# Soft mixture layer: logits computed once with slots on partitions, token maxima from transposed raw tiles, combine weights exponentiated in place later, dispatch turned tile by tile

## What is computed

```python
def _L1_ffn_ref(x, phi, w1, b1, w2, b2):       # x (4, 512, 192), phi (4, 256, 192)
    logits = jnp.einsum('bnd,esd->bnes', x, phi)
    B, N, E, S = logits.shape
    dispatch = jax.nn.softmax(logits, axis=1)
    combine = jax.nn.softmax(logits.reshape(B, N, E * S), axis=-1).reshape(B, N, E, S)
    slots = jnp.einsum('bnd,bnes->besd', x, dispatch)
    h = jax.nn.gelu(jnp.einsum('besd,edh->besh', slots, w1) + b1[None, :, None, :])
    y = jnp.einsum('besh,ehd->besd', h, w2) + b2[None, :, None, :]
    out = jnp.einsum('besd,bnes->bnd', y, combine)
    return out
...
t = t + _L1_ffn_ref(_ln_t(t), phi, w1, b1, w2, b2)
```

## Time and profile before

| | us |
|---|---|
| median of three runs | 1077.12 |
| the three runs | 1083.49, 1074.96, 1077.12 |
| the profiled execution | 1087.93 |
| its span on the core | 1086.2 |

### The profile page before, as it was taken

One profiled execution on the slowest core, in us unless ns is written; L12 is line 12 of the kernel. 1 busy time (PEld: TensorE's weight loads), 2 busy tenths in 40 slices (PEclk: granted clock), 3 DMA queues, 4 the chain that ended last, 5 costly groups with the idle time before them and its releaser, 6 DMA issues.

```text
span 1086.2 us, 15072 instructions
## 1 busy us (share of the span) xinstructions
PE 974.2 (90%) x5552; PEld 772.5 (71%) x5552; DVE 530.0 (49%) x1021; ACT 470.3 (43%) x919; POOL 107.7 (10%) x193
## 2 busy tenths in 40 slices
PE   3788878888888887999989889999999999999998
PEld 2655665576557555887767676899689967997798
DVE  5767668865877676343354455203520353026200
ACT  6655355563545554332244345332542164216321
POOL 3012002100400001123142000000000000000000
PEclk9889979996899999998599999999999999999999
DMA  6001000000000001000000020000000000000000
GB/s 170 1 1 34 2 0 10 23 0 0 29 0 1 1 1 33 10 10 20 19 26 13 1 103 1 1 1 14 0 0 0 14 0 0 0 15 1 0 1 15
DMA packets 12709, 15.45 MB, mean 14 GB/s; under 512 B 5313, under 2 KB 10561, under 8 KB 12545
## 3 DMA queue, kind: packets, MB, share of 16 engines
q1 hardware_dynamic: 10656, 9.46, 2.9%
q0 software_dynamic: 2016, 5.51, 1.8%
HBM read 13.39 MB, written 1.57 MB: 14 GB/s over the span
## 4 chain that ended last, share of the span: by engine, by line
PE 70%; DVE 19%; issue 5%; ACT 4%; DMA 1%; SPq 0%; DVEq 0%; POOL 0%; ACTq 0%; POOLq 0%
PE ps L210 22%; PE ps L1299 11%; PE ps L1054 7%; DVE room L564 6%; PE ps L1275 5%; PE ps L1311 4%; DVE area L262 3%; PE ps L1119 3%; PE ps L1035 3%; ACT area L801 2%; DVE nm L553 2%; PE ps L1168 2%; PE ps L933 2%; PE ps L1253 1%; PE ps L953 1%
## 5 line engine op out<-in xcount | busy, mean ns | idle before, releaser
L210 PE MATMUL ps<-xs,ws 128*128 128x512 f32 x460 | 122.9, 419 | 12.2 <-DVE xs L473 8.1
L564 DVE RECIPROCAL room<-ps 32x224 f32<-32x224 f32 (+1 forms) x72 | 97.1, 1348 | 70.5 <-PE ps L1054 55.1
L1299 PE MATMUL ps<-area 128*128 128x192 f32 x768 | 127.4, 326 | 0.0
L1299 PEld LDWEIGHTS ps<-area 128*128 128x128 f32 x768 | 124.9, 190 | 2.0
L210 PE MATMUL ps<-ws,wx 128*128 128x512 f32 x480 | 116.0, 397 | 1.2 <-DVE ws L689 1.2
L699 DVE TENSOR_TENSOR area<-ps,area 128x384 f32<-128x384 f32 x32 | 17.8, 558 | 196.4 <-PE ps L1299 196.4
L210 PEld LDWEIGHTS ps<-xs,ws 128*128 128x128 f32 x460 | 89.3, 200 | 33.9 <-issue 9.3
L801 ACT ACTIVATE area<-ps,nm 112x196 f32<-112x196 f32 (+1 forms) x240 | 85.6, 435 | 60.7 <-DVE nm L553 60.7
L210 PEld LDWEIGHTS ps<-ws,wx 128*128 128x128 f32 x480 | 89.2, 188 | 22.6 <-DVE ws L689 2.9
L905 ACT ACTIVATE area<-ps,bcol 128x512 f32<-128x512 f32 x96 | 65.6, 688 | 86.6 <-PE ps L210 86.5
L1054 PE MATMUL ps<-area,room 98*64 98x224 f32 x384 | 88.9, 378 | 12.0 <-DVE area L569 12.0
(11 more groups left out here) (148 smaller groups left out, 1407.4 us busy)
## 6 DMA issues: line engine op xcount, KB each, us to landing
stage<-in_wall POOLq DMA_DIRECT2D x42, 128.0 KB, 2.4
area<-in_w2e SPq DMA_DIRECT2D x1, 2304.0 KB, 8.4
out<-xres SPq DMA_DIRECT2D x4, 384.0 KB, 2.6
xres<-in_x SPq DMA_DIRECT2D x1, 1152.0 KB, 7.1
area<-in_wall SPq DMA_DIRECT2D x2, 512.0 KB, 6.1
area<-in_w2a SPq DMA_DIRECT2D x1, 576.0 KB, 4.0
room<-in_rel SPq DMA_DIRECT2D x4, 128.0 KB, 5.5
xres<-in_x SPq DMA_DIRECT2D x1, 384.0 KB, 3.1
```

Of the source, the lines that this page charges most:

```text
L210: last = mm(out_, l, r, start=n == 0, stop=n == len(pairs) - 1)
L564: V.reciprocal(dn, ps[32:64, 6, 0:n]).then_inc(a_own, 1)
L1299: last = mm(ps[:, 4 + b, s * D:s * D + D], hTd[:, m, b * T + s * P:b * T + s * P + P], w2x[:, e * MC + m, :], start=m == 0, stop=m == MC - 1)
```

## The change

The token logits are gone. Each slot tile s is computed once, slots on partitions, into banks 0 to 3 in turn, and copied raw to `ct` (ScalarE for even s, VectorE for odd). From there three things go on.

- VectorE takes its two maxima out of SBUF, ScalarE its exponentials into a ring of four `dt_` tiles, VectorE the reciprocals, and GpSimd multiplies. TensorE transposes each tile as it comes, three steps behind its product, into banks 6 and 7, from where VectorE (even) and ScalarE (odd) copy it to `dd`.
- TensorE transposes the raw tile too (banks 4 and 5), and VectorE takes the maxima over its slots (`pm`), then over the tiles (`nrm`, negated). Four more transposes of a broadcast operand spread these maxima over the partitions, and VectorE copies them to `bc`.
- GpSimd adds `bc` to the eight raw tiles, and ScalarE takes their exponentials in place after the last gelu. The row sum comes from a column of ones in `yy`: the last product is 193 columns wide, and VectorE takes the reciprocal of that column ahead of the residuals.

The groups of tokens to slots are ordered by slot half; the first one is issued ahead of the last tile's transposes. The removed lines of the `body_d` functions are left out here, since they stand in the functions above.

```diff
-        (cc, _, ct, dt_, w2x, b2row) = views([(2, NE * NS), (1024,), (ST, N), (2, ST, T), (NE * MC, D), (NE, D)])
-        dd = cc, dt_[:, 0].rearrange("p s t -> p (s t)").rearrange("p (j c) -> p j c", j=2)
-        yy = area[:, 0:2 * ST * D].rearrange("p (b s d) -> p b s d", b=2, d=D)
-        dstart = 2 * NE * NS + 1024 + ST * N
-        hTd = area[:, dstart:dstart + MC * N].rearrange("p (a b) -> p a b", b=N)
+        (dd, dt_, _, ct, bc, w2x, b2row) = views([
+            (2, 2, NE * NS), (4, 2, T), (ST * 2,), (ST, N), (N,), (NE * MC, D), (NE, D)])
+        yy = area[:, 0:2 * ST * (D + 1)].rearrange("p (b s d) -> p b s d", b=2, d=D + 1)
+        hTd = area[:, 2 * ST * (D + 1):2 * ST * (D + 1) + MC * N].rearrange("p (a b) -> p a b", b=N)
...
+            def dispatch_combine(n):
+                for s in range(ST):
+                    pool.wait_ge(d_rc, n * ST + s + 1)
+                    nc.gpsimd.tensor_tensor(dt_[:, s % 4], dt_[:, s % 4],
+                                            rcs[:, 2 * s:2 * s + 2].unsqueeze(2).broadcast_to([P, 2, T]), ALU.mult)\
+                        .then_inc(d_dn, 1)
+                pool.wait_ge(d_bc, n + 1)
+                for s in range(ST):
+                    nc.gpsimd.tensor_tensor(ct[:, s, :], ct[:, s, :], bc, ALU.add).then_inc(d_cs, 1)
...
                 for n in range(PAIRS):
+                    if ph == 3 and n:
+                        dispatch_combine(n - 1)
...
+            dispatch_combine(PAIRS - 1)
...
+                for s in range(ST + 3):
+                    if s < ST:
+                        if s % 2:
+                            dve.wait_ge(d_l, it * ST + s + 1)
+                            V.tensor_copy(ct[:, s, :], ps[:, s % 4, :]).then_inc(d_rv, 1)
+                        dve.wait_ge(d_rv if s % 2 else d_ra, it * 4 + s // 2 + 1)
+                        V.tensor_reduce(ncm[:, 2 * s:2 * s + 2], ct[:, s, :].rearrange("p (b t) -> p b t", b=2),
+                                        AX.X, ALU.max, negate=True).then_inc(d_ncm, 1)
+                    if 1 <= s <= ST:
+                        v = s - 1
+                        dve.wait_ge(d_dt, it * ST + v + 1)
+                        V.reciprocal(rcs[:, 2 * v:2 * v + 2], csum[:, 2 * v:2 * v + 2]).then_inc(d_rc, 1)
+                        dve.wait_ge(d_rt, it * ST + v + 1)
+                        V.tensor_reduce(pm[:, :, v], ps[:, 4 + v % 2, :].rearrange("p (n c) -> p n c", c=P),
+                                        AX.X, ALU.max).then_inc(d_pm, 1)
+                    if s == ST:
+                        dve.wait_ge(d_pm, it * ST + ST)
+                        V.tensor_reduce(nrm[:], pm, AX.X, ALU.max, negate=True).then_inc(d_nm, 1)
+                    if s >= 4 and s % 2 == 0:
+                        dve.wait_ge(d_dtr, it * ST + s - 3)
+                        V.tensor_copy(dd[:, :, :, (s - 4) * P:(s - 3) * P],
+                                      ps[:, 6 + s % 2, :].rearrange("p (b j c) -> p b j c", b=2, c=P)).then_inc(d_de, 1)
+                dve.wait_ge(d_bt, it + 1)
+                V.tensor_copy(bc, ps[:, 4, :]).then_inc(d_bc, 1)
+                for h in range(2):
+                    for b in range(2):
+                        dve.wait_ge(d_sh, it * 4 + 2 * h + b + 1)
+                        bank = 4 * h + 2 * b
...
-                        V.tensor_tensor(yy[:, b, 2 * e:2 * e + 2, :],
+                        if e + b == 0:
+                            V.memset(yy[:, :, :, D:D + 1], 1.0)
+                        V.tensor_tensor(yy[:, b, 2 * e:2 * e + 2, 0:D],
                                         ps[:, 4 + b, 0:2 * D].rearrange("p (s d) -> p s d", d=D),
...
+                        front_split(it + (3 * PAIRS + 1), NT, (d_l, ST * it + ST))
+                for k in range(2):
+                    dve.wait_ge(d_o, 1 + it * 2 + k + 1)
+                    po = ps[:, 6 + k, 0:2 * (D + 1)].rearrange("p (t c) -> p t c", c=D + 1)
+                    V.reciprocal(rrs[:, 2 * k:2 * k + 2], po[:, :, D]).then_inc(d_own, 1)
+                    dve.wait_ge(d_own, it * 2 + k + 1)
+                    for t in range(2):
+                        xt_ = xres[:, it * NT + 2 * k + t, :]
+                        V.scalar_tensor_tensor(xt_, po[:, t, 0:D], rrs[:, 2 * k + t:2 * k + t + 1], xt_,
+                                               ALU.mult, ALU.add).then_inc(d_res, 1)
...
+                for s in range(ST + 4):
+                    if s < ST:
+                        if s % 2 == 0:
+                            act.wait_ge(d_l, it * ST + s + 1)
+                            A.activation(ct[:, s, :], ps[:, s % 4, :], ACT.Copy).then_inc(d_ra, 1)
+                        act.wait_ge(d_ncm, it * ST + s + 1)
+                        if s >= 4:
+                            act.wait_ge(d_dtr, it * ST + s - 3)
+                        for b in range(2):
+                            last = A.activation(dt_[:, s % 4, b, :], ct[:, s, b * T:b * T + T], ACT.Exp,
+                                                bias=ncm[:, 2 * s + b:2 * s + b + 1],
+                                                accum_out=csum[:, 2 * s + b:2 * s + b + 1])
+                        last.then_inc(d_dt, 1)
+                    if s >= 4 and s % 2:
+                        act.wait_ge(d_dtr, it * ST + s - 3)
+                        A.activation(dd[:, :, :, (s - 4) * P:(s - 3) * P],
+                                     ps[:, 6 + s % 2, :].rearrange("p (b j c) -> p b j c", b=2, c=P), ACT.Copy)\
+                            .then_inc(d_da, 1)
+                for h in range(2):
+                    for b in range(2):
+                        act.wait_ge(d_st, 1 + it * 4 + 2 * h + b + 1)
+                        bank = 4 * h + 2 * b
...
+                for s in range(ST):
+                    act.wait_ge(d_cs, it * ST + s + 1)
+                    A.activation(ct[:, s, :], ct[:, s, :], ACT.Exp).then_inc(d_ce, 1)
...
+                def to_slots(b, h):
+                    for part in range(2):
+                        for j in range(2):
+                            last = mm(ps[:, 4 * h + 2 * b + part, :], xn[:, 2 * b + j, part * P:part * P + P],
+                                      dd[:, b, j, 512 * h:512 * h + 512], start=j == 0, stop=j == 1)
+                    last.then_inc(d_st, 1)
+                for s in range(ST + 3):
+                    if s < ST:
+                        if s >= 4:
+                            pe.wait_ge(d_rv if s % 2 else d_ra, it * 4 + s // 2 - 1)
+                        product(ps[:, s % 4, :], (CPHI + s * P, CPHI + s * P + P), xcols(0, N)).then_inc(d_l, 1)
+                    if 1 <= s <= ST:
+                        v = s - 1
+                        pe.wait_ge(d_rv if v % 2 else d_ra, it * 4 + v // 2 + 1)
+                        if v >= 2:
+                            pe.wait_ge(d_pm, it * ST + v - 1)
+                        for n in range(NT):
+                            last = tr(ps[:, 4 + v % 2, n * P:n * P + P], ct[:, v, n * P:n * P + P], ident[:])
+                        last.then_inc(d_rt, 1)
+                    if s >= 3:
+                        v = s - 3
+                        if v == 0:
+                            pe.wait_ge(d_res, 1 + it * NT)
+                        pe.wait_ge(d_dn, it * ST + v + 1)
+                        if v >= 2:
+                            pe.wait_ge(d_da if v % 2 else d_de, it * 4 + v // 2)
+                        for n in range(NT):
+                            last = tr(ps[:, 6 + v % 2, n * P:n * P + P],
+                                      dt_[:, v % 4, n // 2, n % 2 * P:n % 2 * P + P], ident[:])
+                        last.then_inc(d_dtr, 1)
+                    if s == ST + 1:
+                        pe.wait_ge(d_de, it * 4 + 2)
+                        pe.wait_ge(d_da, it * 4 + 2)
+                        gated(pe, 0)
+                        to_slots(0, 0)
...
+                pe.wait_ge(d_nm, it + 1)
                 for n in range(NT):
-                    turn_dispatch(n, range(ST - 2, ST) if n < 2 else range(ST)).then_inc(d_dtr, 1)
+                    last = tr(ps[:, 4, n * P:n * P + P], nrm[:, n:n + 1].broadcast_to([P, P]), ident[:])
+                last.then_inc(d_bt, 1)
+                to_slots(1, 0)
+                pe.wait_ge(d_bc, it + 1)
+                pe.wait_ge(d_de, it * 4 + 4)
+                pe.wait_ge(d_da, it * 4 + 4)
+                gated(pe, 0)
...
-                        last.then_inc(d_st, 1)
+                    to_slots(b, 1)
                 pe.wait_ge(ld_w2, 32)
                 pe.wait_ge(w_split, NCHUNK - QKV_CHUNKS)
-                pe.wait_ge(d_ss, 1 + it * 4 + 3)
+                pe.wait_ge(d_ss, 1 + it * 4 + 2)
...
+                        if n == 0:
+                            pe.wait_ge(d_ce, it * ST + s + 1)
                         if n == 0 and s == ST - 2:
                             pe.wait_ge(d_ye, 1 + it * 2 * NE + 2 * NE)
```

(29 more changed lines are left out.)

104 lines of the change are left out of this document (10 added, 94 removed).

## The result

The changed kernel took 1071.91 us (median of 20 runs, 1063.47 to 1094.17). The ratio is 0.9895 with an interval of 0.9865 to 0.9925: a gain of 1.05%, some 11.4 us, where 17.2 us were forecast. Ratios with an interval leave disturbed runs out, so they are not always the quotient of two medians.

A forecast was written before the change was run, and what follows sets the result against it. TensorE was taken to bound the front; 4.4 us saved a pass, 17.4 for four, less 0.2 at the end, made 17.2 us off the 1077.12 median: 1060 us, range 1046 to 1080.

The forecast's parts named there:

- TensorE bounds the front: First 27.50 us of a pass (logits, exponentials, transposes): TensorE busy 26.37; removing 40 matmuls takes 9.5 us off it.
- The walk: Slot tiles followed through eleven steps, each engine in written order: TensorE waits in the front, first token-to-slot group at 22.2 us.
- Groups, spread and last transposes without a wait: After the front: 13.34 us of groups plus 0.9 run to 36.4 us, against 40.8 before; gain 4.4 a pass.
- Hidden parts: GpSimd's additions, late exponentials, table load and residuals: off the path, except 0.17 us for the reciprocal at the very end.
- Rival A: Whole pass: the walked waits hold, gain 4.4 us a pass, 1060 us (bounds 1052 to 1066); chance 0.54.
- rival B: Token-to-slot matmuls: TensorE's clock halves for some 3.5 us, losing 1.8 us a pass, 7 in all, 1067 us; chance 0.20.
- C: Front's middle through the four groups: clock stays at half, 12 us a pass lost, 1125 us; chance 0.13.
- D: Front: the waits are absent, a pass reaches expert products at 30.2, gain 10.6 us a pass, 1035 us; chance 0.08.
- E: Front: a longer wait than the bounds, from slow GpSimd or a misread order, 1070 to 1085 us; chance 0.05.

The follow-up runs named there:

- e6: The changed kernel with each logits product issued twice into the same bank, putting the 40 removed matmuls back as useless ones; 1102.59 us, ratio 1.022 to the kernel before.
- e2: The changed kernel with useless matmuls in TensorE's waits ahead of dispatch tiles 4, 5 and 6; 1066.38 us, ratio 0.9833 to the kernel before.
- e11: The changed kernel with the same instructions in another order on VectorE, ScalarE and TensorE; 1037.79 us, ratio 0.9543 to the kernel before.

## Why the prediction was wrong in size

Step by step, as the prediction put them.

- *TensorE bounds the front, a removed matmul is worth its time only if TensorE does not wait instead*: right. It did wait, and e6 puts the worth at 5.9 of 9.5 us.
- *The walk, first group at 22.2 us*: right. Measured 22.04 to 22.17 where the clock held in the front; place, order and releaser of the five long waits as named. Their sizes are each 0.2 to 0.4 below the walk's, but most of that is the way of counting: the walk counts from where the next matmul might start, the profile from a modelled end, which by the walk's own durations is 0.16 to 0.18 later. Single durations were off in both directions: handoffs shorter (GpSimd starts 0.08 after the reciprocal in place of 0.2), and two exponentials out of SBUF 1.00 us to the next in place of 0.90. That they cancelled out is luck. The multiplication took 1.04 us in place of 1.5, which by the walk moves nothing:

```profile
858.93 0.51 ACT L892 ACTIVATE area<-area,dstat 128x256 f32<-128x256 f32 x1 [1.48 <-DVE dstat L678]
859.34 0.19 ACT L892 ACTIVATION_READ_ACCUMULATOR area<-area,dstat 128x1 f32 x1
859.44 0.49 ACT L892 ACTIVATE area<-area,dstat 128x256 f32<-128x256 f32 x1
859.93 0.57 ACT L899 ACTIVATE area<-ps 128x512 f32<-128x512 f32 x1
```

  Out of PSUM one exponential and its sum read had taken 0.45 to the next, here 0.51 and 0.49. The rule of the Trainium skill, page "VectorE: DVE Perf Modes", "The TRN2 errata", weighed there at 0.04 us each, agrees: 0.04 to 0.06 more. A VectorE reduction out of SBUF took the same 0.69 as out of PSUM.
- *Groups, spread and last transposes without a wait, 36.4*: no wait, right. 36.25 where the clock held.
- *Hidden parts* (GpSimd's additions, 9.87 us where 12 were taken; late exponentials; table load; residuals): all hidden. The last product took 0.10 us more in each pass, twice the 0.05 forecast, and the reciprocal at the end is there at 0.17.
- *Rival A, the walk holds, the likeliest at 0.54; rival B, the clock falls shortly, 0.20*: **this is the step that failed.** The sum put the lost clock at nothing and took the dense groups at 0.417 us a matmul. B had the mechanism, the place and the price: half clock for 3.4 us, for the most part in the first dense group, 1.7 us a pass where 1.8 was worked out, but in three passes of four. B's sum, 17.2 less 7, is 10; the profile shows 12.3 and the runs 11.4. With the waits filled (e2) the clock stayed at 1.00 and the gain was 17.3, where A's sum had 17.2: the rest of the sum was right in total. What was held against B, that the front of before never lost its clock, was no evidence for a front that has waits of 4.5 us in place of 1.1, the longest near its end. The prediction saw the 5.3 us with only 2.2 us of work, and then weighed an old trace without such a place above, which had one.
- *Rivals C, D, E*: none came. C's long low clock is absent (back within 3.4 us each time); D is what e11 reaches with another order (30.2, the very number of D), but not this kernel.
- *The base*: the forecast was taken off 1077.12, a median of three; from the 1084.26 of twenty runs the same 17.2 would give 1067. Of the 11.9 us between 1060 and 1071.91, 7.1 are this base and 4.8 the smaller gain. The time stands inside the range all the same, because B and part of E had been taken into it.

What stays open: why the fall spares some passes, and whether the change shifts the clock in the untouched stages ahead. The same kernel had a granted clock of 0.80 from 500 to 600 us in one profile and 0.71 in another, and the first logits at 629.70 and 641.75.

## What to carry to other kernels

When work is taken out of the engine that bounds a stretch, walk the new waits, and then look for a place where TensorE does little for some microseconds just ahead of dense matmuls: price the clock there as the likely case, and remove the idling by order, or fill it. When a tile passes between two engines in turn, the written order within each (copy of the next tile ahead of the long work on this one) can be worth as much as the work removed (6.0 us a pass here, against 5.9 by e6). Compare short changes by the stretch they touch, since whole times carry the clock of every other stage.

## What was not expected of the hardware

- Ten useless matmuls a pass, put into waits, shorten the stage by 5.0 us (432.86 to 427.83).
- 32 transposes and a wait of 1.63 us kept the clock at 1.00 in four passes; a wait of 4.59 us lost it in four; several waits around transposes, the longest 1.76, lost it in three of four.
- GpSimd's 128x512 multiplication by a broadcast column took 1.04 us and its addition 1.23 us (eight in a row in 9.87), less than twice the 0.765 us of the 128x256 row.
